# The last group's expert results are scattered to the tokens instead of being fetched by them

## What is computed

```python
logits = xf @ Wg
topw, topi = jax.lax.top_k(logits, TOP_K)            # 2 of 8 experts per token
topw = jax.nn.softmax(topw, axis=-1)
comb = comb.at[jnp.arange(N)[:, None], topi].add(topw)
gu = jnp.einsum('nd,edh->enh', xf, Wgu) + bgu[:, None, :]
g, u = jnp.split(gu, 2, axis=-1)
h = jax.nn.silu(g) * u
eo = jnp.einsum('enh,ehd->end', h, Wd) + bd[:, None, :]
out = jnp.einsum('end,ne->nd', eo, comb)             # h + out is the result
```

## Time and profile before

| what | us |
|---|---|
| median of 3 runs (lowest, highest) | 818.74 (817.44, 818.9) |
| the profiled execution's own time | 824.18 |
| its span, first to last instruction | 822.4 |
| PE busy | 603.9 (73%) |
| POOL busy | 498.1 (61%) |
| DVE busy | 430.1 (52%) |
| ACT busy | 264.7 (32%) |

### The profile page before, as it was taken

One profiled execution on the slowest core, in us unless ns is written; L12 is line 12 of the kernel. 1 busy time (PEld: TensorE's weight loads), 2 busy tenths in 40 slices (PEclk: granted clock), 3 DMA queues, 4 the chain that ended last, 5 costly groups with the idle time before them and its releaser, 6 DMA issues.

```text
span 822.4 us, 12791 instructions
## 1 busy us (share of the span) xinstructions
PE 603.9 (73%) x3335; PEld 519.1 (63%) x3335; DVE 430.1 (52%) x1708; ACT 264.7 (32%) x690; POOL 498.1 (61%) x520
## 2 busy tenths in 40 slices
PE   3787645327778788698989986999898969999000
PEld 2687634316567576586878875888787758888000
DVE  4789655343556657265655766355544623445122
ACT  2502122112234432244442543254253324444000
POOL 5602327763655756377677776477777767760674
PEclk9998855557789988698997997899999979999555
DMA  7185000126345533565655663667577768984221
GB/s 152 53 290 148 1 0 26 33 90 186 101 127 153 145 104 106 164 194 150 185 169 154 205 198 106 191 202 218 179 214 235 236 197 257 279 279 147 80 77 61
DMA packets 84597, 125.23 MB, mean 152 GB/s; under 512 B 15044, under 2 KB 57792, under 8 KB 84526
## 3 DMA queue, kind: packets, MB, share of 16 engines
q1 hardware_dynamic: 72526, 101.66, 40.9%
q0 software_dynamic: 11520, 22.35, 9.5%
q10 hardware_dynamic: 480, 0.41, 0.4%
HBM read 84.25 MB, written 43.25 MB: 155 GB/s over the span
## 4 chain that ended last, share of the span: by engine, by line
PE 37%; POOL 21%; DVE 14%; issue 13%; DMA 7%; ACT 3%; SPq 3%; POOLq 0%; DVEq 0%; ACTq 0%
PE gu L587 15%; PE dn L587 11%; POOL gat L1048 8%; POOL xbuf L1034 8%; PE mx L587 5%; POOL rs L966 3%; DMA gat<-ybuf,ypos 3%; PE xTp L765 3%; DMA space<-xbuf 2%; DMA space<-in_x_dram 2%; PE tr L587 2%; ACT x L894 1%; PE tr L719 1%; DVE gat L1485 1%; DVE rec L1268 1%
## 5 line engine op out<-in xcount | busy, mean ns | idle before, releaser
L1034 POOL DMA_INDIRECT xbuf<-x,pos x180 | 186.4, 1035 | 112.9 <-DVE pos L1369 56.0
L587 PE MATMUL gu<-space,wts 128*128 128x256 f32 x912 | 246.0, 410 | 9.1 <-DVE space L1476 9.1
L1476 DVE SCALAR_TENSOR_TENSOR space<-gu,wts,space 128x256 f32<-128x256 f32 x228 | 109.1, 482 | 235.7 <-ACT space L912 173.3
L1048 POOL DMA_INDIRECT gat<-ybuf,ypos x180 | 177.7, 987 | 87.9 <-issue 55.5
L912 ACT ACTIVATE space<-gu,wts 128x256 f32<-128x256 f32 x228 | 109.1, 479 | 305.7 <-PE gu L587 305.3
L587 PEld LDWEIGHTS gu<-space,wts 128*128 128x128 f32 x912 | 174.8, 206 | 32.0 <-DVE space L1476 10.9
L587 PEld LDWEIGHTS dn<-wts,space 128*128 128x128 f32 x912 | 127.9, 204 | 14.1 <-DVE space L1476 7.1
L587 PE MATMUL dn<-wts,space 128*128 128x128 f32 x912 | 129.1, 288 | 5.8 <-DVE space L1476 5.8
L765 PE MATMUL xTp<-cst,space 128*128 128x128 f32 x228 | 51.8, 311 | 40.2 <-DMA space<-xbuf 38.1
L765 PEld LDWEIGHTS xTp<-cst,space 128*128 128x128 f32 x228 | 26.7, 154 | 52.6 <-DMA space<-xbuf 40.8
L966 POOL TENSOR_TENSOR rs<-ve,nhalf 128x4 f32<-128x4 f32 (+2 forms) x39 | 40.4, 1036 | 29.7 <-DVE ve L1281 15.2
(11 more groups left out here) (198 smaller groups left out, 837.8 us busy)
## 6 DMA issues: line engine op xcount, KB each, us to landing
wts<-wall SPq DMA_DIRECT2D x114, 386.0 KB
space<-xbuf SPq DMA_DIRECT2D x114, 128.0 KB, 2.6
ybuf<-space SPq DMA_DIRECT2D x114, 128.0 KB
xbuf<-zero_rows SPq DMA_DIRECT2D x4, 1024.0 KB, 10.5
xt<-in_txt_dram SPq DMA_DIRECT2D x16, 256.0 KB, 3.0
xbuf<-zero_rows SPq DMA_DIRECT2D x32, 128.0 KB
out_dram<-gat SPq DMA_DIRECT2D x16, 256.0 KB
xbuf<-x,pos POOLq DMA_INDIRECT x180
```

The lines of the kernel that those rows point to most:

```text
L587: return nc.tensor.matmul(o, l, r, start=a, stop=z_)
L1034: nc.gpsimd.indirect_dma_start(out=xbuf, out_offset=bass.IndirectOffsetOnAxis(pos[0:p, c:c + 1], 0), in_=x2[n % NX2][0:p, m // 2 * D:(m // ...
L1048: nc.gpsimd.indirect_dma_start(out=gat[b][0:p, (k * W4 + j) * D:(k * W4 + j + 1) * D], out_offset=None, in_=ybuf[g], in_offset=bass.Indire ...
L1476: V.scalar_tensor_tensor(hid[q % 4], gu_ps[q % 3][:, SLOT:2 * SLOT], wts[k % NW][:, W_B + HT + t:W_B + HT + t + 1], sil[q % 3], ALU.add, A ...
```

## The change

It concerns the last group (chunks 18 to 22, tiles 87 to 113) and what it needs elsewhere:

- A row of `xbuf` has 130 numbers now instead of 128, in all groups: the token's vector, the weight of its expert, and the number of a row in a new DRAM tensor `results`. Only chunks 18 to 22 fill the last two. `x2` has a second half for the second choice's rows: ACT copies the vectors there (`x_copy`), and DVE writes the row numbers and the weights (`weights`).
- `row_keep` multiplies a result row by its weight for tiles of the last group: two ACT instructions of 128 columns instead of one of 256. `store_tile` does nothing there; instead POOL sends the tile's rows to `results` with two indirect DMAs (`scatter_rows`), two tiles behind the one being multiplied. The 40 gathers of the last group are gone. `load_results` (SP) reads each chunk's 1,024 rows with one plain DMA of 512 KB, and `combine` is two wide additions on DVE.
- Spare and padding rows need row numbers too, so that they land in places of their own. POOL writes these into `zero_rows` (`number_pads`), which is 8 times as large as before and 2 columns wider per row: one set of numbers before the spare rows are written, and another once they have landed.
- `NX` grows from 5 to 8, `NG` and `NXT` shrink from 4 to 3, and some semaphores are merged.

```diff
+SCATTERED = (len(GROUPS) - 1,)
+ROW = D + 2
+A_CHUNK = P * W4 * 2
+SENT_BACK = [n for g in SCATTERED for n in range(*GROUPS[g])]
+SPARE_ROW = len(SENT_BACK) * A_CHUNK
+PAD_ROW = SPARE_ROW + E * SLOT
+RESULT_ROWS = PAD_ROW + E * SLOT
...
-GATHER_TO = TILE_TO[1:] + [TILE_TO[-1] + GATHER_LAG + 16]
+GATHER_TO = TILE_TO[1:] + [GATHER_FROM[-1] + 2 * (GROUPS[-1][1] - GROUPS[-1][0])]
-NX = 5
+NX = 8
-NG = 4
-NXT = 4
+NG = 3
+NXT = 3
...
+LOAD_PAIRS = [p for g in SCATTERED for p in spread(list(range(*GROUPS[g])), GATHER_FROM[g], GATHER_TO[g])]
...
-    xbuf = nc.dram_tensor("xbuf", (ROW0[-1], D), F32, kind="Internal").ap()
+    xbuf = nc.dram_tensor("xbuf", (ROW0[-1], ROW), F32, kind="Internal").ap()
...
-        zero_rows = sb("zero_rows", [P, SUB * D])
+        zero_rows = sb("zero_rows", [P, E * SUB * ROW])
+        place0 = sb("place0", [P, W4 * 2], I32)
...
+            sp.wait_ge(W.spare_ok, 1)
             for g in range(len(GROUPS)):
                 sp.dma_start(xbuf[ROW0[g] + E * CAP[g]:ROW0[g + 1], :].rearrange("(e p s) d -> p e (s d)", e=E, s=SUB),
-                             zero_rows[:, :].unsqueeze(1).to_broadcast([P, E, SUB * D])).then_inc(W.spare, 16)
+                             zero_rows[:, :].rearrange("p (e c) -> p e c", e=E)).then_inc(W.spare, 16)
             for n in range(IMG_CHUNKS, FIRST + AT["text_load"][0]):
...
+                sp.wait_ge(W.spare_ok, 2)
+                for e, row in enumerate(rows):
+                    sp.dma_start(xbuf[bass.ds(row, SLOT), :].rearrange("(p s) d -> p (s d)", s=SUB),
+                                 zero_rows[:, e * SUB * ROW:(e + 1) * SUB * ROW]).then_inc(W.padded, 16)
...
-                sp.dma_start(xrow[k % NX].rearrange("p (s d) -> p s d", s=SUB),
-                             xbuf[bass.ds(row, SLOT), :].rearrange("(p s) d -> p s d", s=SUB)).then_inc(xrow_in[k % NX], 16)
+                if k >= NX and tile_group(k - NX) in SCATTERED:
+                    sp.wait_ge(yrow_sent[(k - NX) % NYB], rows_sent_before(k - NX))
+                sp.dma_start(xrow[k % NX], xbuf[bass.ds(row, SLOT), :].rearrange("(p s) d -> p (s d)", s=SUB)
+                             ).then_inc(xrow_in[k % NX], 16)
                 wait(sp, W.dn_ok, k - NW + 1)
...
             def store_tile(k):
+                g = tile_group(k)
+                if g in SCATTERED:
+                    return
                 sp.wait_ge(W.y_row_ok, k + 1)
...
+            def load_results(n):
+                b, g = n % NG, group_of(n)
+                if n == GROUPS[g][0]:
+                    for m in range(TILE0[g + 1] - NYB, TILE0[g + 1]):
+                        sp.wait_ge(yrow_sent[m % NYB], rows_sent_before(m))
+                if n - NG < GROUPS[g][0]:
+                    sp.wait_ge(gat_out[b], out_before(n - NG))
+                else:
+                    sp.wait_ge(W.sum_ok, n - NG + 1)
+                r0 = SENT_BACK.index(n) * A_CHUNK
+                sp.dma_start(gat[b], results[r0:r0 + A_CHUNK, :].rearrange("(p q) d -> p (q d)", p=P)).then_inc(xt_in[b], 16)
...
+                if sent_back(n):
+                    sp.dma_start(out[n - IMG_CHUNKS, T_IMG:T, :].rearrange("(p j) d -> p (j d)", j=W4), h1_of(n)).then_inc(gat_out[b], 16)
+                    return
...
+            def x_copy(n):
+
+                act.wait_ge(W.x2_ok, n + 1)
+                rows = x2[n % NX2][:, :].rearrange("p (k j c) -> p k j c", k=2, j=W4)
+                copy(rows[:, 1, :, 0:D], rows[:, 0, :, 0:D]).then_inc(W.copy_ok, 1)
...
-                    act.wait_ge(yrow_out[k % NYB], stored_before(k - NYB))
-                copy(yrow[k % NYB], dn_ps[k % 2][:, 0:SUB * D]).then_inc(W.y_row_ok, 1)
+                    if tile_group(k - NYB) in SCATTERED:
+                        act.wait_ge(yrow_sent[k % NYB], rows_sent_before(k - NYB))
+                    else:
+                        act.wait_ge(yrow_out[k % NYB], stored_before(k - NYB))
+                if tile_group(k) not in SCATTERED:
+                    copy(yrow[k % NYB], dn_ps[k % 2][:, 0:SUB * D]).then_inc(W.y_row_ok, 1)
+                    return
+                for s in range(SUB):
+                    last = nc.scalar.activation(yrow[k % NYB][:, s * D:(s + 1) * D], dn_ps[k % 2][:, s * D:(s + 1) * D], ACT.Copy,
+                                                scale=xrow[k % NX][:, s * ROW + D:s * ROW + D + 1])
+                last.then_inc(W.y_row_ok, 1)
 
...
+                j, k = divmod(m, 2)
+                if sent_back(n) and m == 0:
+                    pool.wait_ge(W.meta_ok, SENT_BACK.index(n) + 1)
+                    pool.wait_ge(W.w1_ok, n + 1)
+                    pool.wait_ge(W.copy_ok, SENT_BACK.index(n) + 1)
...
+            def scatter_rows(k):
+
+                pool.wait_ge(W.y_row_ok, k + 1)
+                for s in range(SUB):
+                    place = xrow[k % NX][:, s * ROW + D + 1:s * ROW + D + 2].bitcast(I32)
+                    nc.gpsimd.indirect_dma_start(out=results, out_offset=bass.IndirectOffsetOnAxis(place, 0),
+                                                 in_=yrow[k % NYB][:, s * D:(s + 1) * D], in_offset=None
+                                                 ).then_inc(yrow_sent[k % NYB], 16)
+
+            def number_pads(base):
+                ids = zero_rows[:, :].bitcast(I32).rearrange("p (e s c) -> p e s c", e=E, s=SUB)[:, :, :, D + 1]
+                return nc.gpsimd.iota(ids, [[SLOT, E], [1, SUB]], base=base, channel_multiplier=SUB)
+
+            pool.wait_ge(W.zero_ok, 1)
+            pool.wait_ge(W.x2_zero, NX2 + 3)
+            number_pads(SPARE_ROW).then_inc(W.spare_ok, 1)
+            pool.wait_ge(W.spare, 16 * len(GROUPS))
+            number_pads(PAD_ROW).then_inc(W.spare_ok, 1)
...
+                    for k, t in units(i, s):
+                        if t == 1 and tile_group(k) in SCATTERED:
+                            if k - 2 >= TILE0[tile_group(k)]:
+                                scatter_rows(k - 2)
+                            if last_of_group(k):
+                                scatter_rows(k - 1)
+                                scatter_rows(k)
...
+            V.tensor_copy(ones_r[:, :], one[:, :].to_broadcast([P, P])).then_inc(W.index_ok, 1)
             V.memset(zero_rows[:, :], 0.0).then_inc(W.zero_ok, 1)
+            V.memset(pos[:, :], 0.0).then_inc(W.x2_zero, 1)
+            for v in x2:
+                V.memset(v[:, :], 0.0).then_inc(W.x2_zero, 1)
...
                 wait(dve, W.w0_ok, n)
                 w0, w1 = [w2[0:p, (n * 2 + k) * W4:(n * 2 + k) * W4 + w] for k in range(2)]
+                if sent_back(n):
+                    meta = x2[n % NX2][:, :].rearrange("p (k j c) -> p k j c", k=2, j=W4)
+                    w0, w1 = [meta[:, k, :, D] for k in range(2)]
+                    dve.wait_ge(W.x2_ok, n + 1)
+                    wait(dve, W.w1_ok, n)
+                    V.tensor_scalar(meta[:, :, :, D + 1].bitcast(I32), place0[:, :].rearrange("p (k j) -> p k j", k=2),
...
+                if not sent_back(n):
+                    dve.wait_ge(gat_in[b], gathered_before(n))
+                else:
+                    dve.wait_ge(xt_in[b], results_before(n))
+                    h = h1_of(n).rearrange("p (j d) -> p j d", d=D)
+                    both = gat[b].rearrange("p (j k d) -> p j k d", k=2, d=D)
+                    V.tensor_tensor(both[:, :, 0], both[:, :, 0], both[:, :, 1], ALU.add).then_inc(W.half_ok, 1)
+                    dve.wait_ge(W.half_ok, n + 1)
+                    V.tensor_tensor(h, h, both[:, :, 0], ALU.add).then_inc(W.sum_ok, 1)
+                    return
```

More of the change, by code:

```diff
@@ L279, in program @@
         top[0] = 6 * ROWS
-        xrow = [part(SUB * D) for _ in range(NX)]
+        xrow = [part(SUB * ROW) for _ in range(NX)]
         xT = [part(SLOT) for _ in range(2)]
@@ L387, in program @@
         yrow_out = [sem(f"s_yrow_out{i}") for i in range(NYB)]
+        yrow_sent = [sem(f"s_yrow_sent{i}") for i in range(NYB)]
         gat_in = [sem(f"s_gat_in{i}") for i in range(NG)]
@@ L425, in stored_before, with rows_sent_before, results_before @@
         def stored_before(k):
-            return 16 * (k // NYB + 1)
+            return 16 * sum(tile_group(m) not in SCATTERED for m in range(k % NYB, k + 1, NYB))
+        def rows_sent_before(k):
+            return 16 * SUB * sum(tile_group(m) in SCATTERED for m in range(k % NYB, k + 1, NYB))
         def gathered_before(n):
             return 16 * sum(2 * width(m) for m in range(n % NG, n + 1, NG))
+        def results_before(n):
+            return 16 * (len(range(n % NG, B, NXT)) + sum(1 for m in SENT_BACK if m <= n and m % NG == n % NG))
         def out_before(n):
@@ L577, in _ @@
                         store_out(n)
+                    for n in loads(i, s):
+                        load_results(n)
                     for g in opens(i, s):
@@ L938, in _ @@
                         x_norm(chunk_of("x_norm", i))
+                    if due("x_copy", i, s) and sent_back(chunk_of("x_copy", i)):
```

(1 more changed line is left out.)

69 lines of the change are left out of this document (35 added, 34 removed).

## The result

| | median | runs | profiled execution | its span | granted clock |
|---|---|---|---|---|---|
| before | 818.82 us | 817.44 to 820.21 | 824.18 us | 822.4 us | 0.835 |
| after | 868.15 us | 865.72 to 870.03 | 870.03 us | 868.2 us | 0.811 |

The ratio is 1.0589 (95%: 1.0552 to 1.0626). The change costs 49 us; 853 us (834 to 872) was predicted, +34. The spans differ by 45.8; the other 3.5 come from which execution was profiled, since before's lay 5.4 above its median and after's 1.9.

What follows compares the result with a forecast made beforehand. PE bounded the stage before the end, POOL the end; POOL would bound the last stage. Span 822.4 - 60.9 (old end) + 58.9 (POOL's later end) + 21 (tail) + 15 (start) = 856.4, 34 more; on the median 853 us (834 to 872).

Steps and rivals of the forecast that it cites:

- tiles at the lower clock: Upper end of the range, 872: a third to three quarters of the last group's tiles with PE at its lower clock.
- all terms at their upper bounds: Other way to the range's upper end, 872: start, scatter and tail all at their upper bounds.
- POOL becomes the limit of the last stage: Last group's 27 tiles: 54 scatters and 56 gathers take POOL 140.1 us, 5.2 per tile against PE's 3.29.
- POOL's head start is lost: Before the last stage: third group's gathers wait behind the first result row, losing 15 us; POOL starts at 680.3.
- The start costs 15: Ahead of chunk 0's `norm2`: POOL waits until four spare-row DMAs have landed, 15 us.
- The tail of 21: After POOL's last DMA: last gather, combine, store, result loads and sums to the end, 21 us (bounds 15 and 25).
- The rival of the lower clock: Last stage: PE, idling behind POOL, falls to its lower clock, 6.3 us a tile; 879, or 866 for half; chance 0.13.
- Rows of 130 numbers move worse: Tile loads and scatters of all groups: if a quarter slower, 4 to 8 us in all, 860; chance 0.06.
- Edits at nothing: Small edits elsewhere cost nothing: DVE zeroing at most 1 us, POOL's extra wait for weights at most 0.6 a chunk.
- start absent: Spare rows' wait falls under other work, leaving only 19 us more: 838; chance 0.12.
- tail at its lower bound: After POOL's last DMA: tail of 15 us if the loads overlap fully; part of the range's lower end.

Runs made afterwards that it cites:

- e6: Changed kernel with each of the 54 scatters of result rows issued twice, the second time into another DRAM tensor: 935.05 us, ratio 1.1414.
- e7: Changed kernel with one gather instead of eight for each of group 2's seven chunks, 49 DMAs fewer, results not the reference's: 807.98 us.
- e2: Changed kernel with 12 of group 2's 56 gathers issued on POOL ahead of the first scatter of result rows: 857.24 us, ratio 1.0446.
- e1: Changed kernel with POOL writing the first spare-row numbers and signalling SP before the image stage instead of right ahead of its main loop: 851.37 us, ratio 1.0348.
- e3: Changed kernel with DVE working out each chunk's two weights ahead of its places instead of behind them: 868.42 us, ratio 1.0553.
- e4: Kernel before with the change's three instead of four buffers for gathered rows and for text chunks: 822.64 us, ratio 1.0006.

## Why the prediction was right, and where it was off

The measured 868 is in the upper part of the range, and not for the reasons that its upper end was made of (tiles at the lower clock, or all terms at their upper bounds). The mechanism came as forecast; the 15 us that are missing come from elsewhere, as told below.

- **POOL becomes the limit of the last stage: right, shown.** 140.1 us for 110 DMAs forecast, 141.9 measured, 5.3 for a tile instead of 5.2; 54 more cost 67 (e6), 49 fewer gave the stage back to PE (e7). The scatters cost 1.29 as taken from the earlier trace rows. The gathers came to 0.983 + 0.30 = 1.29 instead of the 1.26 of the earlier trace rows, and make up the 1.8.
- **POOL's head start is lost: right, shown.** It stood idle for 17.16 us, and filling 15.1 of them with 12 gathers brought 11.2 (e2).
- **The start costs 15: right.** The wait was 14.80, and taking it away brought 17 to 20 (e1). SP's weight copies were held until 147 (146 forecast) and nothing waited for them: e1's first scatter is back at before's time, and its later waits are the others'.
- **The tail of 21: 20.2 measured.** The store and the loads followed each other as worked out. Two misses nearly cancel: the last sum ended 17.7 us after POOL's last DMA instead of 16.6, and what follows it took 2.5 instead of 4.5.
- **The rival of the lower clock: half of it happened.** PE did fall to 0.72 in parts of the stage, and to 0.69 in e6. The timeline of PE around one wait:
```profile
726.53 1.03 PE L643 MATMUL gu<-space,wts 128*128 128x256 f32 x4
730.86 2.08 PE L643 MATMUL gu<-space,wts 128*128 128x256 f32 x4 [3.29 <-DVE space L1590]
...
734.85 1.89 PE L643 MATMUL gu<-space,wts 128*128 128x256 f32 x8
```
  Four matmuls took 1.03 us ahead of the wait and 2.08 behind it, and the next tile's eight are back at the upper level with 1.89. What fell is the price. I had let every tile of that clock last 6.3 us, but a PE that has a backlog works without waits and comes back as here. So it lost a few us out of its own idle time, and POOL's next row was always there. The loss that the Trainium skill describes (TensorE: Matmul & The Clock Gate, "HAM oscillation — how this bites in real kernels") is in the records; on the time it had no effect that shows, because PE was not the limit.
- **Rows of 130 numbers move worse: fallen.** The issue group of tile loads reads as in the earlier trace rows:
```profile
space<-xbuf SPq DMA_DIRECT2D x114, 130.0 KB, 2.6
```
  The scatters to `xbuf` are no slower either: 1.028 us each now, 1.035 before. By the Trainium skill (DMA: Bandwidth & Descriptors, "How a descriptor splits into AXI transactions") a descriptor that doesn't start on a multiple of 256 bytes can take more transactions; no row here counts them. At this size, and with 0.38 to 0.65 of the DMA engines' time in use in the four stretches above, no difference in time shows. The prediction's reason, a DMA share of "0.87 at its fullest", misread, where the stretch from 43.7 us has 1.01.
- **The step that was too small: "Edits at nothing".** I put POOL's extra wait for the weights at 0.6 us a chunk at most. It was 3.5 at chunk 18 and 3.2 to 3.9 at chunk 22, with only part won back: 5.4 us on the first result row of the changed kernel, and about as much or more in e1, e3, e6 and e7, together with the 0.6 for ACT's second instruction and the hand-over that the forecast did have. That the wait is all of it is not shown (e4). In the trace of before DVE worked out chunk 22's places at 638.39 and its weights only at 640.84, with a wait for ACT and a tile's operation between them, and POOL's scatter had gone off at 639.63:
```profile
638.39 0.22 DVE L1369 TENSOR_REDUCE pos<-spot 128x8 int32<-128x64 f32 x1
639.95 0.48 DVE L1476 SCALAR_TENSOR_TENSOR space<-gu,wts,space 128x256 f32<-128x256 f32 x1 [1.34 <-ACT space L912]
...
640.84 0.16 DVE L1347 TENSOR_TENSOR w<-ex,w 128x4 f32<-128x4 f32 x1
```
  The rows that size this wait stood in that trace, 2.4 us apart; the forecast counted the operations and not when they run.
- **The rest.** Of the 15 us between forecast and median (868.15 - 853), 4.8 are this wait (5.4 less 0.6), 1.8 the gathers, 3.5 the choice of execution, with 0.8 the other way for the tail. What is left, 6 us, is two spreads that I had read as if they were fixed: the image stage's end (about 2) and the stretch up to chunk 17's first scatter (about 4). Why that stretch varies from 357 to 367 us between executions is not settled; for the same 1,411 matmuls the granted clock was 0.81 before (127 to 487 us) and 0.79 after (144 to 508).
- **A slip in the range.** Its lower end, start absent and tail at its lower bound, is 853 - 15 - 6 = 832 by the prediction's own terms, not 834. Nothing hangs on it here.

## What to carry to other kernels

Price an indirect DMA as a fixed slot on POOL and count slots by stage, before asking what its bytes cost: moving them off the tail is worth nothing if the stage that takes them is thereby filled beyond what the bounding engine needs. Where a helper engine has idle time ahead of a wait, put the work that is ready first, but leave it something to do between rows. And when a step gains one more input, look at when that input is ready in the old trace, not at how long it takes to compute; a cheaper way to a shorter tail may be to move a boundary, as one line of group limits did here.

## What the runs showed of the hardware

- POOL's price for an indirect DMA of 128 rows of 512 bytes hardly depends on what goes on beside it: 1.26 (gathers alone), 1.29 (mixed), 1.283 (164 in a row, a third of them writing a second tensor). 0.30 of it is issue between two of them.
- Four writes of 1,040 KB from one tensor in SBUF, issued over 5.65 us, had landed 14.8 us after the first, 0.29 MB per us, with nothing beside them but SP's next copies.
- A PE that is held back by another engine is granted less clock (1.00 before, 0.83 over the stage after, 0.72 in e6), and gets it back when the waits go (0.98 in e7).
